# Three layers of attention on one core: self attentions in pairs between cross attentions, projections for two batches at once, tasks placed by a table

## The chip, the cores and the metric

The kernel runs on one core of a Trainium2 chip. The metric is the time of one execution in microseconds (us), on the device, as the median of several runs. A core has five engines that run side by side, each with its own instruction stream in order: TensorE (PE in the profile, with PEld for its weight loads), VectorE (DVE), ScalarE (ACT), GpSimd (POOL) and SyncE (SP), which here only starts DMAs. They meet at semaphores.

## The reference, cut to what matters

There are 8 batches of 112 tokens with 256 channels, and for each batch a context of 375 tokens. Everything is float32. One layer of cross attention is followed by a block with self attention, a second cross attention and an MLP.

```
# layer 0                                  16 heads of 16, softmax over 375 keys
xq, xkv = ada_ln(x, cond), ada_ln(ctx, cond)
x = x + mha(xq @ Wq + bq, k, v) @ Wp + bp          # k, v = xkv @ Wkv + bkv
# layer 1                                  self attention, 112 keys
h = ln(x) * (1 + scale_msa) + shift_msa            # shift, scale, gate = silu(cond) @ ada_w + ada_b
x = x + gate_msa * (mha(q, k, v) @ self_o_w + self_o_b)   # q, k, v = h @ qkv_w + qkv_b
# layer 2                                  cross attention, ctx is not normalised
x = x + mha((ln(x) * g2 + b2) @ q_w + q_b, k, v) @ cross_o_w + cross_o_b
# MLP, hidden 1024
x = x + gate_mlp * (gelu((ln(x) * (1 + scale_mlp) + shift_mlp) @ w1 + b1) @ w2 + b2)
```

Batches don't meet anywhere: batch b of layer 2 needs only batch b of layer 1, and so on.

## The kernel before, in words

**Attentions and steps.** There are 24 attentions: number i is layer i // 8, batch i % 8, and they run in that order, so the eight self attentions (8 to 15) stand in one block. `ORDER` (L58) is the list of steps that all five engine programs walk through: 3 x 12 steps ahead of attention 0 (FIRST = -3), then 12 steps for each cross attention and 4 for each self attention. In step u of attention i TensorE computes one unit of scores (`scores_t`, 4 matmuls, L477), ScalarE takes its exponential (`exponential`, L709, with the maximum already inside the product), and some steps later TensorE multiplies with the values (`values`, L522). Units share two PSUM banks, so unit n + 2 waits for the exponential of unit n.

**What an attention needs first.** The float32 product of queries and keys is made from bfloat16 parts: three parts each, six products stacked to a depth of 96, and three further rows that hold the negated maximum. So ahead of each attention comes a chain: the row maxima (`scores` L496 and L500 on TensorE, `maximum` L933 and L935 on VectorE: 16 for a cross attention, 4 for a self attention, two PSUM banks in turn), then `chain` (L943 to L949) that splits them, fill "N" (L603, L974) that transposes them, and a DMA by `load_maxima` (L1237) into the three rows of `q_stack`. The first unit of the attention waits for that DMA. For cross attentions `chain` is in step 8 and "N" in step 9 of the attention before; for self attentions in steps 0 and 1 of the attention before.

**Fills.** All other TensorE work between two attentions is cut into fills, each in one of two PSUM banks in turn (`fill`, `read`): "T" transposes half of a context, "K" projects half of its keys (L571, 375 columns), "V" its values (L577; two fills, of two and one blocks of 125 tokens), "X" transposes a normalised x, "Q" and "KS" project queries and self-attention keys of one batch (L594, 8 matmuls of 112 columns), "VS" self-attention values (L600), "A" and "B" prepare modulations and biases. The steps of the fills are written out by hand in tables (`NORM_AT`, `X_AT`, `Q_AT`, `T_AT`, `K_AT` and so on, L73 to L143).

**Jobs.** What "Q" and "KS" make is one job each, 32 in all: ScalarE writes it to `job_full` (L769), GpSimd splits it in four instructions (`split_job`, L1151 to L1157), and SyncE stacks it with six DMAs (`load_job`, L1232). Keys of a context go the same way (`split_keys` L1142 and L1144, `load_keys` L1222, 12 DMAs for an attention).

**Normalisation.** VectorE computes mean and variance (`norm` L924, L927; `context_stats` L911, L916), GpSimd the reciprocal root and the normalised rows (`norm` L1131 to L1137, `norm_context` L1118 to L1125).

**Start.** silu(cond) is computed on 8 partitions (`silu` L888 to L892), transposed by TensorE (L450) and used in L459; ScalarE starts all 17 small bias DMAs before its first activation. GpSimd waits for the bias rows (L1103) before it normalises anything.

**Other DMAs.** ScalarE's queue starts the contexts (`load_context`, L815, mostly in step 6 of an attention) and the weights; `wq`, `wkv` and `wo` are one buffer for layers 0 and 2.

**End.** After the last attention come the MLP's matmuls (`first_matmuls` L631, `second_matmuls` L641) for four pairs of batches.

Of the kernel before, what the change touches and what calls it, by code (L numbers as in the profile page):

```python
# [13 lines left out]
P = 128  # L14
# [19 lines left out]
QB = H * T + P - T  # L34
# [6 lines left out]
NA = 3 * B  # L41
FIRST = -3


def cross(i):
    return not B <= i < 2 * B


def steps(s):
    return 4 if B <= s < 2 * B else 12  # L50


def units(i):
    return 12 if cross(i) else 4


UNIT0 = [sum(units(j) for j in range(i)) for i in range(NA + 1)]
ORDER = [(s, u) for s in range(FIRST, NA) for u in range(steps(s))]  # L58

# [6 lines left out]
def cidx(i):  # L66
    return i if i < B else i - B


CROSS = [i for i in range(NA) if cross(i)]  # L70


NORM_AT, X_AT, Q_AT, KS_AT, VS_AT = {}, {}, {}, {}, {}  # L73
for p_, n_, x_, q_ in zip(range(B),
# [3 lines left out]
    NORM_AT[p_], X_AT[p_], Q_AT[p_] = n_, x_, q_  # L78
for b_ in range(B):
    p_ = B + b_  # L80
    if b_ < 6:
        NORM_AT[p_] = (b_ + 1, 10) if b_ else (2, 0)
        X_AT[p_], Q_AT[p_], KS_AT[p_], VS_AT[p_] = (b_ + 2, 3), (b_ + 2, 6), (b_ + 2, 8), (b_ + 2, 11)
    else:
        NORM_AT[p_] = (7, 10) if b_ == 6 else (9, 1)
        s_ = 8 if b_ == 6 else 10
        X_AT[p_], Q_AT[p_], KS_AT[p_], VS_AT[p_] = (s_, 0), (s_, 1), (s_, 2), (s_, 3)
    p_ = 2 * B + b_
    if b_ < 5:
# [12 lines left out]

T_AT, K_AT, V_AT = {}, {}, {}
for i_ in CROSS:
    T_AT[i_] = [(i_ - 3, 9), (i_ - 3, 10)]
    K_AT[i_] = [(i_ - 2, 0), (i_ - 2, 2)]
    V_AT[i_] = [(i_ - 1, 4), (i_ - 1, 5)]
T_AT[16], K_AT[16], V_AT[16] = [(9, 0), (9, 2)], [(11, 2), (11, 3)], [(12, 2), (12, 3)]
T_AT[17], K_AT[17] = [(13, 2), (13, 3)], [(14, 1), (14, 2)]
T_AT[18] = [(15, 1), (15, 2)]  # L110
STATS_AT = {i: [(i - 4, 8), (i - 4, 9), (i - 4, 10)] for i in range(B)}
STATS_AT[0] = [(-3, 1), (-3, 2), (-3, 3)]
XNC_AT = {i: (i - 3, 5) for i in range(B)}


MAX_AT, CHAIN_AT, N_AT = {}, {}, {}
for i_ in range(NA):
    if i_ == 2 * B:
        MAX_AT[i_] = [(14, k // 3) for k in range(12)] + [(15, 0)] * 4
        MAX_AT[i_] = [(13, 2), (13, 2), (13, 3), (13, 3)] + [(14, k // 3) for k in range(12)]  # L120
        CHAIN_AT[i_], N_AT[i_] = (15, 0), (15, 1)
    elif cross(i_):
        MAX_AT[i_] = [(i_ - 1, k // 2) for k in range(H)]
        CHAIN_AT[i_], N_AT[i_] = (i_ - 1, 8), (i_ - 1, 9)
    elif i_ == B:
        MAX_AT[i_], CHAIN_AT[i_], N_AT[i_] = [(7, k) for k in range(4)], (7, 4), (7, 5)
# [1205 lines left out]
```

## Time and profile before

| what | us |
|---|---|
| median of 3 runs (577.23 to 582.75) | 579.2 |
| the profiled execution, its own time | 582.22 |
| its span, first to last instruction | 580.4 |
| TensorE busy in the span | 467.1 |
| ahead of attention 0 | 80.87 |
| attentions 0 to 7 | 193.7 |
| self attentions 8 to 15 | 94.75 |

The profile is of one execution. Its own time is 1.8 us above its span and 3.0 us above the median of the runs. The attention stretches are read from the first L477 of each attention in the timeline: 80.87, 274.57 and 369.32 us.

### The profile page before, as it was taken

To read this page: it belongs to the slowest core of one execution; us is meant where nothing else is said; L and a number is where in the kernel's file an instruction comes from. 1 tells how busy PE (TensorE), PEld (TensorE's weight loads), DVE (VectorE), ACT (ScalarE), POOL (GpSimd) and SP (SyncE) were. 2 spreads that over 40 slices of the span, in tenths; PEclk is the share of its full clock that TensorE was granted. 3 is DMA by queue.
4 is the path that set the end of the run, shared out by engine and by line. 5 is a ranking of instruction groups with operands and counts; after the bars stand their busy time and mean duration, and the time that the engine had idled before them with its cause. 6 is when DMAs were issued, how large, how long until landed. Compare 5 with 4: busy or idle time off the path is not lost.

```text
span 580.4 us, 11962 instructions
## 1 busy us (share of the span) xinstructions
PE 467.1 (80%) x4446; PEld 342.5 (59%) x4446; DVE 255.4 (44%) x682; ACT 244.6 (42%) x537; POOL 262.1 (45%) x406
## 2 busy tenths in 40 slices
PE   0554769696989999968787866999699998989996
PEld 0432547464656676657665654666466655659885
DVE  0521713445455555535354475546266556622112
ACT  0121132343555655545453343555355555466220
POOL 5444642887585573443446535644223423143000
PEclk9995857888799999998797899899899999799999
DMA  8723421323243434342522422424613231100001
GB/s 207 179 61 95 130 77 29 100 70 81 75 130 96 123 93 110 88 126 81 137 75 58 107 53 64 131 52 124 176 43 96 52 82 46 38 2 1 17 16 33
DMA packets 74786, 48.70 MB, mean 84 GB/s; under 512 B 38968, under 2 KB 71696, under 8 KB 74728
## 3 DMA queue, kind: packets, MB, share of 16 engines
q1 hardware_dynamic: 65804, 38.08, 25.4%
q10 hardware_dynamic: 8924, 9.85, 5.8%
q8 instruction: 36, 0.59, 0.4%
q14 instruction: 22, 0.18, 0.1%
HBM read 17.27 MB, written 0.93 MB: 31 GB/s over the span
## 4 chain that ended last, share of the span: by engine, by line
PE 60%; DVE 11%; DMA 9%; POOL 8%; issue 5%; SPq 4%; ACT 2%; ACTq 0%; POOLq 0%; DVEq 0%
PE bank L571 9%; DMA q_stack<-nm_t 8%; DVE nmax L933 7%; PE bank L522 7%; PE bank L577 7%; PE bank L477 6%; PE bank L496 6%; PE bank L594 6%; PE bank L641 5%; PE bank L631 4%; PE bank L543 3%; POOL ctx_norm L1125 3%; PE bank L531 2%; POOL x_norm L1137 1%; SPq L873 1%
## 5 line engine op out<-in xcount | busy, mean ns | idle before, releaser
L933 DVE TENSOR_REDUCE nmax<-bank 112x1 f32<-112x375 f32 x256 | 127.9, 543 | 157.4 <-PE bank L496 157.2
L709 ACT ACTIVATE prob<-bank 125x448 f32<-125x448 f32 (+1 forms) x224 | 120.1, 544 | 136.4 <-PE bank L477 119.9
L477 PE MATMUL bank<-q_stack,k_stack 99*128 99x112 bf16 x768 | 73.0, 222 | 24.3 <-DMA q_stack<-nm_t 16.2
L496 PE MATMUL bank<-k_stack,q_stack 96*128 96x375 bf16 x256 | 75.2, 346 | 17.5 <-DVE nmax L933 8.1
L477 PEld LDWEIGHTS bank<-q_stack,k_stack 99*128 99x128 bf16 x768 | 52.0, 103 | 48.4 <-DMA q_stack<-nm_t 19.5
L571 PE MATMUL bank<-ctx_t,wkv 128*128 128x375 f32 x128 | 59.7, 599 | 2.8 <-ACT ctx_t L730 1.8
L496 PEld LDWEIGHTS bank<-k_stack,q_stack 96*128 96x128 bf16 x256 | 25.6, 102 | 54.9 <-DVE nmax L933 34.2
L1131 POOL TENSOR_SCALAR x_veps<-x_mv 112x1 f32<-112x1 f32 x32 | 7.4, 233 | 105.7 <-DVE x_mv L927 105.2
L522 PE MATMUL bank<-prob,v_tokens 125*17 125x112 f32 x1536 | 52.2, 271 | 0.1
L1142 POOL CAST k_parts<-k_rest 128x375 bf16<-128x375 f32 x32 | 16.0, 499 | 79.3 <-DVE k_rest L983 79.3
L577 PE MATMUL bank<-wkv,ctx_t 128*125 128x256 f32 x192 | 49.9, 397 | 0.0
L522 PEld LDWEIGHTS bank<-prob,v_tokens 125*17 125x17 f32 x1536 | 34.7, 100 | 15.9 <-issue 12.9
L1137 POOL TENSOR_SCALAR x_norm<-x_tokens,x_mv,x_rstd 112x256 f32<-112x256 f32 x32 | 39.6, 1237 | 3.3
L935 DVE TENSOR_REDUCE nmax<-bank 112x4 f32<-112x448 f32 x32 | 19.8, 624 | 41.4 <-PE bank L500 41.2
L577 PEld LDWEIGHTS bank<-wkv,ctx_t 128*125 128x125 f32 x192 | 34.9, 195 | 4.2
L571 PEld LDWEIGHTS bank<-ctx_t,wkv 128*128 128x128 f32 x128 | 26.7, 231 | 15.9 <-issue 6.0
L1151 POOL CAST job_part<-job_full 128x224 bf16<-128x224 f32 x32 | 12.1, 378 | 52.8 <-ACT job_full L769 52.7
L739 ACT ACTIVATE k_parts<-bank,bias_heads 128x375 bf16<-128x375 f32 x32 | 18.4, 575 | 36.5 <-PE bank L571 36.5
L1125 POOL TENSOR_SCALAR ctx_norm<-ctx_tokens,ctx_mv,ctx_rstd 125x256 f32<-125x256 f32 x24 | 29.6, 1242 | 0.8
L1144 POOL TENSOR_TENSOR k_parts<-k_rest,k_parts 128x375 bf16<-128x375 f32 x32 | 27.3, 852 | 2.6
L641 PE MATMUL bank<-late_space,k_self_stack 128*112 128x256 f32 x128 | 28.1, 379 | 0.0
L769 ACT ACTIVATE job_full<-bank,bias_heads 128x112 f32<-128x112 f32 x64 | 19.2, 352 | 19.3 <-PE bank L594 19.2
(114 smaller groups left out, 753.4 us busy)
## 6 DMA issues: line engine op xcount, KB each, us to landing
k_stack<-k_parts SPq DMA_DIRECT2D x192, 93.8 KB, 2.2
q_stack<-job_part SPq DMA_DIRECT2D x144, 56.0 KB, 2.0
ctx_tokens<-in_ctx_dram ACTq DMA_DIRECT2D x14, 375.0 KB
k_self_stack<-job_part SPq DMA_DIRECT2D x48, 56.0 KB, 2.0
late_space<-in_L_xcond_mlp_w_dram ACTq DMA_DIRECT2D x2, 1024.0 KB, 5.3
late_space<-in_L_xcond_ada_w_dram SPq DMA_DIRECT2D x1, 1536.0 KB, 6.2
gate_self<-gate_rows SPq DMA_DIRECT2D x8, 112.0 KB, 3.7
k_self_stack<-gate_rows SPq DMA_DIRECT2D x1, 896.0 KB, 7.0
```

The source lines that it names most:

```text
L477: last = pe.matmul(sh.score_t[n % 2][:, j * T:(j + 1) * T], keys, sh.q_all[:, b, o:o + T], start=True, stop=True)
L496: last = pe.matmul(bank[:, 0:L], sh.q_all[0:DEEP, b, place(k) * T:place(k) * T + P], sh.k_st[i % 2][0:DEEP, k, 0:L], start=True, stop=True)
L522: last = pe.matmul(sh.pv[32 * j:32 * j + D + 1, g * T:(g + 1) * T], v, sh.prob[n % NPROB][0:rows, j * T:(j + 1) * T], start=t == 0, stop=t ...
L571: last = pe.matmul(cx[:, 0:L], w[:, c, n * P:(n + 1) * P], sh.ct[i % 2][:, c, :], start=c == 0, stop=c == CH - 1)
L577: last = pe.matmul(cx[0:KT, (t % 2) * C:(t % 2 + 1) * C], sh.ct[i % 2][:, c, t * KT:(t + 1) * KT], sh.wkv[i // B][:, c, C:2 * C], start=c ...
L594: last = pe.matmul(cx[:, m * T:(m + 1) * T], sh.wq[i // B][:, c, at + m * P:at + (m + 1) * P], sh.xt[i % 2][:, c, :], start=c == 0, stop=c ...
L641: last = pe.matmul((sh.pv, sh.tb)[j][0:T, 0:C], sh.hid[p % 2][:, m, j * T:(j + 1) * T], sh.w2[:, m, :], start=m == 0, stop=m == NH - 1)
L709: act.activation(sh.prob[n % NPROB][0:rows, :], sh.score_t[n % 2][0:rows, 0:GH * T], ACT.Exp, scale=SCALE).then_inc(sg.exp_done, 1)
L933: dve.tensor_reduce(sh.nmax[i % 2][:, place(k):place(k) + 1], sh.score[n % 2][0:T, 0:L], AX_X, ALU.max, negate=True).then_inc(sg.max_done, 1)
L1125: pool.tensor_scalar(sh.xnc[:, t, :], sh.ctx[r][:, t, :], sh.ctx_mv[:, j, t, 0:1], sh.ctx_rstd[:, j, t:t + 1], ALU.subtract, ALU.mult).the ...
L1137: pool.tensor_scalar(sh.xn[j][:, :], sh.x[:, b, :], sh.mv[:, j, 0:1], sh.rstd[:, j:j + 1], ALU.subtract, ALU.mult).then_inc(sg.xn_done, 1)
L1144: pool.tensor_tensor(sh.kp[par][:, 2, m, :], sh.kr[:, m, :], sh.kp[par][:, 1, m, :], ALU.subtract).then_inc(sg.split[m], 1)
```

## The change

The order of the attentions becomes a list, `SEQ`. Steps are numbered by one integer g: 17 ahead of the first attention (`PRE`) instead of 36, then 12 or 4 for each as before. The hand-written tables give way to functions: `put` fixes a task in a step, `lightest` picks in a given range of steps the one with the least TensorE time by a table of costs (`LOAD`), and `spread_sp` deals the DMAs of a job or of keys out two to a step. "Q" and "KS" take two batches at once: 16 jobs in place of 32, each twice as wide (224 columns), the two batches side by side in `q_stack`. "V" is three fills of one block. The normalised x (all of it) and the first two contexts move from GpSimd to VectorE. Contexts are loaded 2 or 3 steps after the buffer is free; silu is computed transposed from a transposed load of cond; of the small bias DMAs all but four start after the exponential of silu; the first job is stacked from ScalarE's queue. Layers 0 and 2 get their own weight buffers. The MLP's matmuls are as before.

```diff
-QB = H * T + P - T
+QP = H * 2 * T + P - T
...
+SEQ = ([(0, b) for b in range(5)] + [(1, 0), (1, 1), (0, 5), (0, 6), (1, 2), (1, 3), (0, 7)]
+       + [(2, 0), (1, 4), (1, 5), (2, 1), (2, 2), (1, 6), (1, 7)] + [(2, b) for b in range(3, 8)])
...
+PRE = 17
+START = [PRE + n for n in UNIT0]
...
+def lightest(lo, hi, cost, *task):
+
+    g = min(range(lo, hi + 1), key=lambda g: (LOAD[g] + 0.02 * (g - lo), g))
+    return put(g, *task, cost=cost)
...
+    TAIL_AT[i] = [end + 3, end + 5, end + (8 if nxt == 12 else 6)]
...
+    CHAIN_AT[i], N_AT[i] = (12, 13) if i == 0 else (START[i] - 4, START[i] - 3)
...
+for ci in range(2, NC):
+    g = cross_start(ci - 2)
+    k0 = lightest(g + 1, g + 2, 1.27, "K", ci, 0)
+    K_AT[ci] = [k0, lightest(k0 + 2, g + 5, 1.27, "K", ci, 1)]
...
+for lay in (1, 2, 3):
+    for b in sorted(range(B), key=lambda b: POS[lay - 1, b]):
+        i = POS[lay - 1, b]
+        g = NORM_AT[lay, b] = TAIL_AT[i][2] + 1
...
+        X_AT[lay, b] = lightest(g + 3, g + 4, 0.22, "X", (lay, b), 0)
+        if lay < 3 and b % 2:
+            x = max(X_AT[lay, b], X_AT[lay, b - 1])
+            q = Q_AT[lay, b - 1] = lightest(x + 2, x + 3, 1.5, "Q", (lay, b - 1), 0)
+            if lay == 1:
+                ks = KS_AT[lay, b - 1] = lightest(q + 2, q + 4, 1.5, "KS", (lay, b - 1), 0)
...
+def spread_sp(g, *what):
+    for part in range(3):
+        while g >= PRE and SP_LOAD[g] >= 2:
+            g += 1
+        put_sp(g, *what, part)
+    ISSUED[what] = g
...
             for m in range(CH):
                 for c in range(CH):
-                    last = pe.matmul(cx[:, m * T:(m + 1) * T], sh.wq[i // B][:, c, at + m * P:at + (m + 1) * P], sh.xt[i % 2][:, c, :],
-                                     start=c == 0, stop=c == CH - 1)
+                    last = pe.matmul(cx[:, m * 2 * T:(m + 1) * 2 * T], sh.wq[lay][:, c, at + m * P:at + (m + 1) * P],
+                                     sh.xt[PAIR_NO[i] % 2][:, c, :], start=c == 0, stop=c == CH - 1)
...
+        if g == 4:
+            act.wait_ge(sg.job_step, 4)
+            for part in range(3):
+                stack_job(act, sh, sg, JOBS[0], part)
...
+    weights_at = {5: (0, "wo"), 9: (2, "stage"), 12: (3, "stage"), START[0] + 3: (1, "wv"), START[0] + 9: (1, "wo"),
+                  START[2] + 5: (4, "stage"), START[2] + 10: (5, "stage"), START[3] + 3: (2, "wv"), START[3] + 8: (2, "wo"),
+                  START[6] + 1: (0, "mlp"), START[7] + 4: (1, "mlp")}
+    for ci in range(2, NC):
+        context_at[T_AT[ci - 2][1] + (3 if ci >= B + 2 or ci < 4 else 2)] = ci
...
+    act.wait_ge(sg.cond_in, 32)
+    act.activation(sh.exp_t[:, :, :], sh.cond_t[:, :, :], ACT.Exp, scale=-1.0).then_inc(sg.exp0, 1)
     small_loads(act, sh, sg, ins)
...
     def norm(p):
+        lay, b = p
+        n = NORM_NO[p]
+        dve.wait_ge(sg.xn_rstd, n + 1)
+        if n >= 3:
+            wait_filled(dve, sg, ("X", NORM_ORDER[n - 3], 0))
+        dve.tensor_scalar(sh.xn[n % 3][:, :], sh.x[:, b, :], sh.mv[:, n % 2, 0:1], sh.rstd[:, n % 2:n % 2 + 1],
+                          ALU.subtract, ALU.mult).then_inc(sg.xn_done, 1)
...
+        for p in NORMS.get(g, []):
+            if NORM_NO[p] >= 2:
+                norm_stats(p)
+        for p in NORMS.get(g - 2, []):
+            if NORM_NO[p] >= 2:
+                norm(p)
...
+        if g == START[NA - 5] + 4:
+            sp.wait_ge(sg.st_psum, max(UNIT0[POS[1, b] + 1] for b in range(4, B)))
             sp.dma_start(sh.gate_m, gate_rows[:, 1, :].partition_broadcast(T)).then_inc(sg.gate_m_in, 16)
```

GpSimd keeps the variance's reciprocal root (`rstd`, in its loop one step after VectorE's statistics), the splitting of keys and jobs, the other six contexts' normalisation, and the bias additions.

## Rows read from the trace of the kernel before

**Rows 1.** The page: busy time of three engines, and the granted clock in 40 slices

```profile
PE 467.1 (80%) x4446; PEld 342.5 (59%) x4446; DVE 255.4 (44%) x682; ACT 244.6 (42%) x537; POOL 262.1 (45%) x406
PEclk9995857888799999998797899899899999799999
```

**Rows 2.** Windows: from:to length, busy (count) of PE, PEld, DVE, ACT, POOL; clock; DMA

```profile
0.00:80.87 80.87, 36.67 (x131) 25.69 (x132) 23.46 (x73) 13.93 (x28) 40.11 (x63) 0.83 0.51 131
80.87:148.25 67.38, 54.67 (x447) 38.64 (x448) 27.37 (x82) 24.93 (x54) 42.90 (x59) 0.78 0.26 69
195.88:217.32 21.44, 20.09 (x219) 14.40 (x220) 11.28 (x28) 12.03 (x27) 13.60 (x21) 1.00 0.40 106
274.57:369.32 94.75, 72.15 (x732) 54.83 (x731) 46.47 (x123) 40.69 (x95) 50.73 (x85) 0.89 0.33 87
454.12:473.46 19.34, 17.78 (x199) 11.86 (x200) 11.16 (x28) 10.54 (x23) 6.83 (x11) 1.00 0.25 63
511.50:522.38 10.88, 9.45 (x183) 6.89 (x184) 1.72 (x5) 7.51 (x17) 5.64 (x9) 1.00 0.01 2
522.38:580.40 58.02, 53.56 (x268) 47.95 (x267) 9.91 (x25) 15.99 (x35) 5.54 (x8) 0.98 0.06 17
```

**Rows 3.** Chain that ended last, its start: from us, for us, what

```profile
17.02 5.68 DMA bias_rows<-in_L_xcond_mlp_b_dram
...
44.77 3.64 POOL ctx_norm L1125 x3
...
51.17 0.60 SPq L1232
...
74.44 6.38 DMA q_stack<-nm_t
```

**Rows 4.** The same chain later: pieces at the full clock, and DMA waits

```profile
190.88 0.94 PE bank L594 x8
...
408.17 5.89 DMA q_stack<-nm_t
...
439.06 1.32 PE bank L571 x4
...
442.62 1.79 PE bank L577 x8
...
450.08 0.70 PE bank L522 x24
451.89 2.19 DMA q_stack<-nm_t
...
529.20 6.81 PE bank L631 x36
```

**Rows 5.** Groups by shape: count, busy us, mean ns, idle before

```profile
L496 PE MATMUL bank<-k_stack,q_stack 96*128 96x375 bf16 x256 | 75.2, 346 | 17.5 <-DVE nmax L933 8.1 <-DMA q_stack<-job_part 2.2 <-DVE nmax L935 1.1
L1137 POOL TENSOR_SCALAR x_norm<-x_tokens,x_mv,x_rstd 112x256 f32<-112x256 f32 x32 | 39.6, 1237 | 3.3
L1144 POOL TENSOR_TENSOR k_parts<-k_rest,k_parts 128x375 bf16<-128x375 f32 x32 | 27.3, 852 | 2.6
L1153 POOL TENSOR_TENSOR job_rest<-job_full,job_part 128x224 f32<-128x224 f32 x32 | 19.6, 612 | 2.6
L1013 DVE TENSOR_SCALAR late_space<-bank,mod 128x112 f32<-128x112 f32 x4 | 1.4, 389 | 9.2 <-PE bank L582 9.2
L888 DVE TENSOR_SCALAR late_space<-late_space 8x256 f32<-8x256 f32 x1 | 0.3, 280 | 14.4 <-ACT late_space L824 14.4
```

**Rows 6.** What TensorE waited for: us in total, times, longest

```profile
PE bank L450 <- DVE late_space L892: 18.4, 1, 18.4
PE bank L477 <- DMA q_stack<-nm_t: 17.4, 13, 4.2
```

**Rows 7.** Timeline, two engines side by side at 26 us

```profile
26.64 4.04 POOL L1125 TENSOR_SCALAR ctx_norm<-ctx_tokens,ctx_mv,ctx_rstd 125x256 f32<-125x256 f32 x3
26.67 0.65 DVE L1039 COPY wkv<-k_self_stack 128x256 f32<-128x256 f32 x2
```

More of the change, by code:

```diff
@@ new lines, with cross_start, put @@
+SELF_NO = {i: n for n, i in enumerate(j for j in range(NA) if not cross(j))}
+PRE = 17
+START = [PRE + n for n in UNIT0]
+END = START[NA]
+STEP_OF = {START[i] + u: (i, u) for i in range(NA) for u in range(steps(i))}
+def cross_start(ci):
+    return START[CROSS[ci]] if ci >= 0 else {-1: 4, -2: 1, -3: 0}[ci]
+LOAD = [0.0] * (END + 40)
+TASKS = {}
+def put(g, *task, cost=0.0):
+    TASKS.setdefault(g, []).append(task)
+    LOAD[g] += cost
+    return g
+def lightest(lo, hi, cost, *task):
+    g = min(range(lo, hi + 1), key=lambda g: (LOAD[g] + 0.02 * (g - lo), g))
+    return put(g, *task, cost=cost)
@@ new lines @@
+for i in range(NA):
+    for u in range(steps(i)):
+        LOAD[START[i] + u] += 0.2
+MAX_AT, CHAIN_AT, N_AT, VALUES_AT, TAIL_AT, K_LAND = {}, {}, {}, {}, {}, {}
+for i in range(NA):
+    end = START[i + 1]
+    if cross(i):
+        VALUES_AT[i] = [[START[i] + 4, START[i] + 7, START[i] + 10, end + 1][u // 3] for u in range(12)]
+    else:
+        VALUES_AT[i] = [[START[i] + 3, end + 1][u // 2] for u in range(4)]
+    for g in sorted(set(VALUES_AT[i])):
+        LOAD[g] += 0.9 if cross(i) else 0.6
+    nxt = steps(i + 1) if i + 1 < NA else 12
+    TAIL_AT[i] = [end + 3, end + 5, end + (8 if nxt == 12 else 6)]
+    for g, cost in zip(TAIL_AT[i], (0.44, 0.2, 0.86)):
+        LOAD[g] += cost
@@ new lines @@
+for i in range(NA):
+    CHAIN_AT[i], N_AT[i] = (12, 13) if i == 0 else (START[i] - 4, START[i] - 3)
+for i in range(NA):
+    for g in range(CHAIN_AT[i] - 8, CHAIN_AT[i]):
+        LOAD[g] += 0.32 if cross(i) else 0.11
+    put(N_AT[i], "N", i, 0, cost=0.1)
+T_AT, K_AT, V_AT, STATS_AT, XNC_AT = {}, {}, {}, {}, {}
+T_AT[0], K_AT[0], V_AT[0] = [0, 0], [1, 2], [9, 10, 11]
+T_AT[1], K_AT[1] = [3, 3], [4, 5]
+for kind, at in (("T", T_AT), ("K", K_AT), ("V", V_AT)):
+    for ci, where in list(at.items()):
+        for n, g in enumerate(where):
+            put(g, kind, ci, n, cost={"T": 0.33, "K": 1.27, "V": 0.86}[kind])
@@ new lines, with invert @@
+B_AT = [7, START[1] + 3, START[4] + 8]
+for n, g in enumerate(B_AT):
+    put(g, "B", n, 0, cost=0.43)
+A_AT = [START[0] + 2, START[0] + 6]
+for n, g in enumerate(A_AT):
+    put(g, "A", n, 0, cost=2.0)
+FILL_RANK = {k: n for n, k in enumerate(("N", "K", "X", "Q", "KS", "VS", "V", "T", "B", "A"))}
+FILLS = {g: sorted(t, key=lambda f: FILL_RANK[f[0]]) for g, t in TASKS.items()}
+FILL_NO = {}
+for g in sorted(FILLS):
+    for f in FILLS[g]:
+        FILL_NO[f] = len(FILL_NO)
+def invert(table, many=False):
+    found = {}
+    for key, where in sorted(table.items(), key=lambda kw: kw[1] if not many else kw[1][0]):
+        for n, g in enumerate(where if many else [where]):
+            found.setdefault(g, []).append((key, n) if many else key)
+    return found
@@ new lines @@
+for g in SP_AT:
+    SP_AT[g].sort(key=lambda w: w[0] != "N")
+for i in range(NA):
+    last = CHAIN_AT[i] - 1
+    if i == 0:
+        MAX_AT[i] = [5 + k // 2 for k in range(H)]
+        continue
+    lay, b = SEQ[i]
+    ready = ISSUED.get(("J", ("Q", (lay, b - b % 2), 0)), 4) + 3
+    if cross(i):
+        ci = CIDX[i]
+        first = max(ISSUED.get(("K", (ci, 0)), 9) + 3, ready)
+        second = max(ISSUED.get(("K", (ci, 1)), 11) + 3, first + 2)
+        MAX_AT[i] = [first + (second - first) * k // HC for k in range(HC)] + \
+            [last - (last - second + 1) * (HC - 1 - k) // HC for k in range(HC)]
+    else:
+        MAX_AT[i] = [last - 3 + k for k in range(4)]
@@ L229 @@
+MAXES, MAX_NO = invert(MAX_AT, True), {}
+for g in sorted(MAXES):
+    for m in MAXES[g]:
+        MAX_NO[m] = len(MAX_NO)
+N_MAX = len(MAX_NO)
 MODS = [1.0, 0.0, 1.0, 0.0, 0.0, 1.0, 0.0, 1.0]
@@ L1147, in split_job @@
         j = JOB_NO[f]
-        full, part = sh.full[j % 2], sh.part[j % 2]
+        full, part = sh.full, sh.part[j % 2]
         wait_read(pool, sg, f)
```

797 lines of the change are left out of this document (377 added, 420 removed), and 3 rows, old and new, of the table CROSS.

## The prediction
> **What bounds the kernel now.** I read four views in this order: the page, the windows by stretch, the chain that ended last, and the groups by shape. The page shows TensorE busy 467.1 of 580.4 us and no other engine above 262 [rows 1]; the slices of granted clock fall below full speed at the start and around the self attentions. The windows say where TensorE isn't well used [rows 2]. A cross attention of layer 2 takes 19.34 us, 17.78 of them busy at the full clock: that stretch is bound by TensorE. But 80.87 us pass before attention 0, with 36.67 busy; attentions 0 and 1 take 67.4 us at a mean clock of 0.78; the eight self attentions and the fills between them take 94.75 us with 22.6 idle and a clock of 0.89. The MLP, 58.0 us, is full. So there is a stretch that can only shrink by less work (TensorE's own), and three that lose time to latency. The chain names what is late at the start: a bias row for GpSimd until 22.70 (17.02 + 5.68), two context normalisations of about 4 us on GpSimd, six stacking DMAs at 0.6 us each, and 6.38 us from the issue of the maxima's DMA to its landing, where the same DMA takes 2.19 later [rows 3, 4].
>
> **Part 1: the start.** Before, TensorE waits 18.4 us for silu [rows 6], because 17 DMA issues stand ahead of ScalarE's exponential. After, four do. The modulations still wait for all small loads, which now are issued later; they landed about 21 us before and I take 24. That holds VectorE's queue (x norm, weight order, second statistics stand behind), so the first context is on TensorE at 25 to 27 us and not at 30.7 (the end of GpSimd's normalisation, 26.64 + 4.04) [rows 7]. Two key halves and the paired query projection at the low clock end near 37.5. The normalisation moved to VectorE is bounded by 0.28 and 0.63 us: L888 reads 280 ns, and L1013 389 ns for 112 columns, up to 0.63 if the whole difference from a tiny instruction (some 0.2) grows with width [rows 5]; I take 0.35. What matters more is that GpSimd splits the first job at once instead of after the second context's 3.64 us, which ended at 48.41, with stacking at 50.6 and landing at 55.7 [rows 3]. A job twice as wide costs GpSimd more: from 224 to 375 columns an instruction grows from 612 to 852 ns [rows 5], 1.6 ns a column, so 970 ns at 448, a factor of 1.58 on 2.2 us: 3.4 us. 37.5 + 0.8 (ScalarE's read) + 3.4 + six issues of 0.6 + 2 landing = 47.5, 8 us earlier. From there 16 maxima at 0.55 us of VectorE (8.8), interleaved with two X, a Q of two batches, V and B, take about 16 us, four maxima of attention 1 stand ahead of the split of attention 0's maxima (+2), and the DMA takes 2.2 instead of 6.4 since no context or weight is loaded beside it. First unit at about 68: 13 us gained. Bounds 62 (modulations ready at once, clock high) and 76 (small loads land at 30).
>
> **Part 2: work on TensorE.** A projection of one batch is 0.94 us; eight matmuls of 224 columns are, by 36 of them in 6.81 us, 1.51 [rows 4]. Two batches cost 1.51 instead of 1.88: 0.37 x 16 = 5.9 us saved; one pair lies in the start, where it only shortens the latency. The three V fills do the same matmuls as two did. Weight buffers of their own remove waits that were not late.
>
> **Part 3: the body, by prices.** I price all that stands between the first unit and the MLP, at the full clock. A cross attention's own units: values 4 x 0.70 [rows 4], scores 12 x 0.25 (eight matmuls in 0.50), tail 1.5, so 7.3; 16 maxima 16 x 0.346 [rows 5] = 5.5; keys 2 x 1.32; values projection 1.79 + 0.92 [rows 4]; T 0.65, X 0.35, N 0.2. With K, V, T, X, N and maxima that is 19.3 for the full stretch, which lasted 19.34 [rows 2]; with the Q, KS and VS of layer 1 it is 22.1, where 21.44 was measured: the prices hold to 3%. After: 16 x 7.3 = 116.8; 15 sets of maxima less ten done in the start, 79; 14 K 37.0; 15 V 40.5; 13 T, 26 X, 23 N 22; 14 paired projections 21.1; 8 VS 7.2; 8 self attentions at 4.6 (values 1.0, scores 1.0, tail 1.5, four maxima 1.1) 36.8; A and B 8.2; 2.9 because the last attention has no fills beside it (10.88 for 7.3, less what overlaps) [rows 2]. Sum 371.5. The same list before is 381, and the stretch from 80.87 to 522.38 took 441.5: 60 us lie in waits and in the low clock.
>
> **Part 4: how much of the 60 goes.** By place: attentions 0 and 1 hold 17 (67.4 against 50 by price), the self stretch 27 (94.75 against 67.8), the rest 16, among them two waits of 5.9 for the maxima's DMA where 2.2 is normal [rows 4]. Why the self stretch is late: maxima, split, transpose, DMA and first unit follow one another within four short steps, and there is too little other work. After, self attentions come in twos with the keys, values and projections of cross attentions around them, the maxima of the second one are made during the cross attention before, and I take 2 us left for each pair, 8 in all. Attentions 0 and 1 keep 6: GpSimd is no longer ahead of every X, but A still needs 6.4 us of TensorE in attention 0. Of the rest 6 stay. SyncE loses 96 of 192 job issues, at 0.64 us with the gap about 61 us of its queue, and the maxima's DMA stands first in its step with at most two issues ahead. Contexts are loaded near step 1 and not 6, away from the maxima's DMA in step 9; `gate_m` goes five steps ahead of it. One collision stays, `w1` (1 MB) in the same step as attention 7's maxima: 3.7 us by the difference of 5.89 and 2.19. Sum 20 left. What is late next is TensorE itself, 17.8 of 19.3 us busy.
>
> **Added waits.** VectorE now waits for GpSimd's root (`rstd`) two steps after its statistics; behind that wait stand the maxima, and TensorE's score banks wait for them. GpSimd needs 0.8 us for the root, but a job (3.4) or a context (3.64 plus its root) can stand ahead. Two steps are about 3.2 us, so I count this as hidden, and its failure is a rival. GpSimd itself is relieved: 39.6 us for x, a quarter of the context rows, and 19 us of the jobs go.
>
> There is a row for interference: GpSimd's three normalisations took 4.04 us beside VectorE's 0.65 us of copies, and 3.64 without [rows 3, 7]. The Trainium skill, "SBUF — State Buffer", section "Who interferes with whom", says that VectorE and GpSimd share a pair of ports, and that a tensor_scalar between SBUF buffers can take it whole while GpSimd stands still, or the other way round. The trace agrees by 0.4 us. By that rule each of the 32 moved norms could cost VectorE up to one GpSimd instruction, which makes the rival with the late VectorE likelier.
>
> **Sum.** 68 + 371.5 + 20 + 58 = 517.5 us of span, 519.3 as the profiled execution (1.8 outside the span), and 3.0 less on the scale of the median: forecast **517**, against 579.2.
>
> **Rivals.**
> - All latency is hidden: 62 + 371.5 + 5 + 58 = 496.5, 496 on the median's scale. For it speaks that every fill finds a step with little load; against it that even the fullest stretch idles 1.6 of 19.3 us. Chance 0.15.
> - The self attentions keep their latency: the four dependent links are the same per attention, and in twos the second has only four steps. If 20 of the 27 us stay in place of 8, and half of the start's gain fails, 517 + 12 + 7 = 536. For it speaks that nothing in the chain of links gets shorter. Chance 0.2.
> - The new order only moves the waits, and the change brings its start and its fewer projections alone: 579.2 - 13 - 6 = 560. For it speaks that maxima and fills still alternate in two banks each. Chance 0.08.
> - Slower: VectorE waits for GpSimd's root at every norm. The price is one GpSimd job ahead, 3.4 us, and the ports; TensorE has two score banks and loses it all. With 28 norms after the start a mean wait of 2.2 us eats the whole gain of 62 us; with 3.4 it is 95, so 612. Against it: only 14 jobs and 6 contexts lie in the body, so few norms can meet one. Chance 0.04.
> - The table doesn't do what it says: key DMAs and jobs, two issues a step, miss the step from which the maxima are placed, and TensorE stands at each. At 3 us for each of 20 attentions the gain is gone: 577. Chance 0.03.
>
> The forecast, within 500 to 530, has 0.5. Its range by itself is 500 to 530; the range for 8 in 10 is **498 to 548**. A measurement of this kernel can tell about 1% from no change: faster by over 1% 0.93, within 1% 0.03, slower 0.04.
>
> **What would show it.** Right: first L477 at 62 to 76 us; projections of 224 columns near 0.19 us each, 128 records less; stretches of a full cross attention near 20 us, a pair of self attentions with the fills near 16; `q_stack<-nm_t` waits of TensorE well below 17.4 us; mean clock above 0.916; TensorE busy about 440 us. Wrong: waits of VectorE for GpSimd's `x_rstd` of more than 20 us in total, a start above 76 us because the small loads land late, or idle of TensorE in the self pairs above 5 us each. If TensorE's busy time doesn't fall although its clock rises, the prices of part 3 were not what it pays.

## Result: slower, and the profile after

The kernel after takes 595.8 us (median of 4 runs, 595.3 to 602.2) against 578.2 for the kernel before beside it on the same chip: ratio 1.033, 95% interval 1.022 to 1.043. The forecast was 517, in a range of 498 to 548. The prediction was wrong, in its sign too. In all times and ratios here and below, executions over 1.5% above the fastest one of the same kernel are left out as slow.

The page of after, with busy time and granted clock, to be held against [rows 1]:

```profile
span 592.6 us, 11515 instructions
...
PE 459.1 (77%) x4316; PEld 333.4 (56%) x4316; DVE 273.9 (46%) x719; ACT 241.2 (41%) x521; POOL 201.8 (34%) x304
...
PEclk9998776979999797999869998898869999899999
```

TensorE lost 8 us of work and GpSimd 60, as the change meant, and the span of the profiled executions grew by 12 (by the medians it is 17.5; before's profiled execution was 4 us above its median). So time went into idle of TensorE. The windows of after (columns as in [rows 2]) say where: ahead of attention 0, attentions 0 and 1, a cross attention of layer 2, all attentions together, the MLP.

```profile
0.00:82.27 82.27, 35.60 (x134) 23.78 (x134) 29.19 (x85) 13.85 (x29) 29.49 (x51) 0.89 0.55 132
82.27:141.66 59.39, 47.81 (x421) 33.03 (x420) 25.79 (x79) 24.02 (x52) 29.37 (x41) 0.84 0.24 66
461.44:482.68 21.24, 18.27 (x208) 13.31 (x206) 12.09 (x30) 11.11 (x26) 8.72 (x13) 1.00 0.24 60
82.27:532.60 450.33, 368.62 (x3894) 260.87 (x3896) 233.54 (x607) 210.37 (x457) 165.16 (x242) 0.91 0.31 82
532.60:592.60 60.00, 54.91 (x294) 48.79 (x294) 11.12 (x27) 16.93 (x36) 7.20 (x12) 1.00 0.05 16
```

The same stretch of all attentions in the kernel before:

```profile
80.87:522.38 441.51, 376.86 (x4048) 268.91 (x4049) 222.02 (x584) 214.70 (x475) 216.43 (x337) 0.92 0.32 84
```

TensorE is busy for 368.62 us between the first unit and the MLP. But it stands still for 81.7 us there (450.33 - 368.62), before 64.7 (441.51 - 376.86). The start didn't get shorter: 82.27 for 80.87. The stretch of layer 2 does the same tasks as the one of before in [rows 2] and one paired query projection more. It takes 21.24 us for 19.34, with 2.97 idle and not 1.56, all at the full clock.

What TensorE waited for, in after (us in total, times, longest):

```profile
PE bank L631 <- DVE x_norm L995: 39.8, 23, 8.2
PE bank L655 <- DVE nparts L1018: 32.5, 22, 2.4
PE bank L508 <- DVE silu_t L947: 17.5, 1, 17.5
PE bank L546 <- DVE nmax L1002: 11.5, 35, 0.6
PE bank L546 <- DMA q_stack<-job_part: 10.9, 2, 10.2
PE bank L550 <- DMA k_self_stack<-job_part: 4.8, 1, 4.8
```

and in before:

```profile
PE bank L603 <- DVE nparts L949: 14.8, 10, 2.6
PE bank L560 <- POOL ctx_norm L1125: 12.2, 2, 7.5
...
PE bank L582 <- POOL x_norm L1137: 6.2, 4, 2.6
```

The wait for the maxima's DMA, 17.4 us in [rows 6], is gone (0.3 in after). Two waits for VectorE took its place: for the normalised x (L631, before L582) 39.8 us for 6.2, and for the split maxima (L655, before L603) 32.5 for 14.8. VectorE itself isn't full, 46%. The timeline of after inside another cross attention of layer 2 shows both. First the norm:

```profile
450.27 0.55 DVE L1002 TENSOR_REDUCE nmax<-bank 112x1 f32<-112x375 f32 x1 [1.42 <-PE bank L546]
...
450.73 0.60 DVE L1051 SCALAR_TENSOR_TENSOR k_rest<-bank,bias_heads,k_parts 128x375 f32<-128x375 f32 x1
...
451.25 0.40 DVE L995 TENSOR_SCALAR x_norm<-x_tokens,x_mv,x_rstd 112x256 f32<-112x256 f32 x1
...
451.80 0.38 PE L631 MATMUL bank<-ident,x_norm 112*128 112x112 f32 x2 [1.18 <-DVE x_norm L995]
```

The root was ready at 449.81 (`x_rstd`, 449.24 + 0.57), and VectorE stood idle for 1.42 us. But its program puts the norm at the end of the step, behind a maximum and the reading of keys that TensorE makes in that same step. When it is done, TensorE has already come to the transpose that needs it, and has lost 1.18 us. Then the chain:

```profile
455.34 1.03 PE L593 MATMUL bank<-wo,ot 128*112 128x256 f32 x4
...
456.41 0.42 DVE L1035 TENSOR_TENSOR gated<-bank,gate_self 112x256 f32<-112x256 f32 x1 [2.15 <-PE bank L593]
...
456.87 0.42 DVE L1037 TENSOR_TENSOR x_tokens<-gated,x_tokens 112x256 f32<-112x256 f32 x1
457.21 0.17 DVE L1012 CAST nparts<-nmax 112x16 bf16<-112x16 f32 x1
...
457.83 0.17 DVE L1018 TENSOR_TENSOR nparts<-nrest,nparts 112x16 bf16<-112x16 f32 x1
458.12 0.10 PEld L655 LDWEIGHTS bank<-ident_bf,nparts 112*48 112x48 bf16 x1 [1.71 <-issue]
458.15 0.21 PE L655 MATMUL bank<-ident_bf,nparts 112*48 112x112 bf16 x1 [1.58 <-DVE nparts L1018]
```

All 16 maxima come from earlier steps; the chain needs nothing from this step. But the table puts the third tail step (`end + 8`) in the step that is also the chain's (`START[i] - 4` is step 8 of 12), and VectorE's loop does the tail before the chain. So the chain waits 2.15 us for an output projection with which it has nothing to do, and TensorE loses 1.58. In the kernel before the tail stood one step ahead, in step 7. The Trainium skill, "Perfetto Trace Analysis", section "Tensor Engine Instruction (MATMUL, LD_WEIGHTS)", says that the queues of VectorE, ScalarE and GpSimd are strict: an instruction doesn't overtake one that waits. The trace agrees: VectorE is idle for 2.15 us, with the chain, whose inputs were there, behind the tail.

The start's chain of after, cut to what matters here (columns as in [rows 3]; of the issues of the small loads two are shown):

```profile
1.20 15.25 DMA cond_t<-in_cond_dram
17.19 0.61 ACTq L920
...
26.21 0.62 ACTq L921
26.87 4.70 DMA norm_b<-in_L_xcond_norm_b_dram
...
52.31 6.59 DMA q_stack<-job_part
```

The condition is now loaded transposed, elements of 4 bytes one by one, and lands at 16.45; before, silu came at 18.97. So silu is only 1.5 us earlier (17.4). But 14 small loads are now issued behind the exponential and the last lands at 31.6, where before they were all there at 21.3. The modulations wait for them.

### The profile page after: what moved, and what is told of

The parts are those of the page before. It is cut to its first block, busy times and chain, and to the rows that moved or that the text cites. A ratio compares the mean times of both kernels' runs of the same rounds, so it can differ in the third digit from the quotient of the medians.

```text
span 592.6 us, 11515 instructions
## 1 busy us (share of the span) xinstructions
PE 459.1 (77%) x4316; PEld 333.4 (56%) x4316; DVE 273.9 (46%) x719; ACT 241.2 (41%) x521; POOL 201.8 (34%) x304
## 2 busy tenths in 40 slices
DMA packets 63022, 48.65 MB, mean 82 GB/s; under 512 B 14928, under 2 KB 59936, under 8 KB 62968
## 3 DMA queue, kind: packets, MB, share of 16 engines
q1 hardware_dynamic: 51116, 37.38, 24.5%
## 4 chain that ended last, share of the span: by engine, by line
PE 64%; DVE 17%; DMA 6%; issue 5%; POOL 3%; ACTq 2%; SPq 2%; ACT 1%; DVEq 0%; POOLq 0%
PE bank L572 8%; PE bank L626 7%; DVE nmax L1002 7%; PE bank L621 7%; PE bank L526 6%; PE bank L546 6%; PE bank L645 5%; PE bank L693 5%; PE bank L683 4%; PE bank L593 3%; DMA cond_t<-in_cond_dram 3%; PE bank L581 2%; DVE x_norm L995 2%; PE bank L652 2%; SPq L1317 2%
## 5 line engine op out<-in xcount | busy, mean ns | idle before, releaser
L1002 DVE TENSOR_REDUCE nmax<-bank 112x1 f32<-112x375 f32 x256 | 131.0, 543 | 170.4 <-PE bank L546 169.0
L546 PE MATMUL bank<-k_stack,q_stack 96*128 96x375 bf16 x256 | 80.7, 353 | 24.4 <-DVE nmax L1002 11.5
L621 PE MATMUL bank<-ctx_t,wkv 128*128 128x375 f32 x128 | 53.9, 549 | 2.7 <-ACT ctx_t L778 1.8
L626 PE MATMUL bank<-wkv,ctx_t 128*125 128x256 f32 x192 | 53.3, 400 | 0.1
L631 PE MATMUL bank<-ident,x_norm 112*128 112x112 f32 x64 | 13.5, 296 | 39.8 <-DVE x_norm L995 39.8
L792 ACT ACTIVATE v_tokens<-bank 125x256 f32<-125x256 f32 x48 | 18.5, 385 | 41.7 <-PE bank L626 41.1
L631 PEld LDWEIGHTS bank<-ident,x_norm 112*128 112x128 f32 x64 | 7.2, 153 | 44.7 <-issue 36.4
L621 PEld LDWEIGHTS bank<-ctx_t,wkv 128*128 128x128 f32 x128 | 24.5, 213 | 13.5 <-issue 4.2
L655 PE MATMUL bank<-ident_bf,nparts 112*48 112x112 bf16 x24 | 5.3, 219 | 32.5 <-DVE nparts L1018 32.5
L693 PE MATMUL bank<-late_space,q_stack 128*112 128x256 f32 x128 | 28.1, 379 | 0.0
L683 PE MATMUL bank<-late_space 128*128 128x224 f32 x128 | 25.3, 353 | 0.0
```

What stands on the lines that cost most here:

```text
L546: last = pe.matmul(bank[:, 0:L], sh.q_all[0:DEEP, b // 2, o:o + P], sh.k_st[CIDX[i] % 2][0:DEEP, k, 0:L], start=True, stop=True)
L621: last = pe.matmul(cx[:, 0:L], w[:, c, n * P:(n + 1) * P], sh.ct[i % 2][:, c, :], start=c == 0, stop=c == CH - 1)
L626: last = pe.matmul(cx[0:KT, 0:C], sh.ct[i % 2][:, c, n * KT:(n + 1) * KT], sh.wkv[0 if i < B else 2][:, c, C:2 * C], start=c == 0, stop=c ...
L631: last = pe.transpose(cx[:, c * T:(c + 1) * T], sh.xn[NORM_NO[i] % 3][:, c * P:(c + 1) * P], sh.ident[0:T, 0:T])
L683: last = pe.matmul((sh.score + sh.score_t)[n % 4][:, 0:2 * T], sh.w1[:, c, m * P:(m + 1) * P], sh.xtm[:, c, 2 * p * T:2 * (p + 1) * T], st ...
L693: last = pe.matmul((sh.pv, sh.tb)[j][0:T, 0:C], sh.hid[p % 2][:, m, j * T:(j + 1) * T], sh.w2[:, m, :], start=m == 0, stop=m == NH - 1)
```

## Experiments

Edits are against the kernel after, if not said otherwise. Times are medians, the interval (95%) is that of the ratio to the kernel before beside it, whose median was 576.3 to 578.3 in the groups of runs.

**One part each: chain, norm, both, small loads.** First VectorE's chain ahead of its tail:

```
-        for i, k in TAILS.get(g, []):
-            tail(i, k)
         for i in CHAINS.get(g, []):
             chain(i)
+        for i, k in TAILS.get(g, []):
+            tail(i, k)
```

> The changed kernel with one edit: in VectorE's step the split of the maxima stands before the attention's tail and not behind it. Theory W (the loss is waits that come from a task's place in an in-order stream; the new table puts the third tail step into the step of the split, so fill N waits for the out-projection): TensorE's wait for nparts at fill N falls from 32.5 us to under 8, no wait takes its place, and the time falls by 15 to 25 us, to about 576. Rival M (the waits only move: some other dependency holds the same step): the wait at N falls, others rise by as much, and the time stays within 5 us of 596. Rival S (all of the loss is the start and the slow small loads): no change.

Measured 569.4 us, ratio 0.987 (0.981 to 0.993): 26.4 us less than after, from the order of two calls. TensorE's wait for `nparts` fell by half, to 16.6 us (12 times), and not under 8 as expected; the wait for `x_norm` grew by 3.7 us, to 43.5. Then VectorE's norm at the head of its step:

```
     for g in range(END):
+        for p in NORMS.get(g - 2, []):
+            if NORM_NO[p] >= 2:
+                norm(p)
         for f in FILLS.get(g, []):
...
-        for p in NORMS.get(g - 2, []):
-            if NORM_NO[p] >= 2:
-                norm(p)
```

> The changed kernel with one edit: VectorE's normalisation of x stands at the head of its step, before that step's maxima, and not at its end, where it waits for TensorE's scores and key fills of the same step. Theory W: TensorE's wait for x_norm at fill X falls from 39.8 us to about 12 (8.2 of it are in the start), the time falls by 15 to 25 us, to about 576; VectorE waits for GpSimd's x_rstd a little more than the 8.9 us of now, under 15. Rival M: the wait turns into one of VectorE for x_rstd (over 25 us) and the time stays within 5 us of 596. Rival S: no change.

Measured 579.3, ratio 1.005 (1.001 to 1.009), 16.5 us less than after. TensorE's wait for `x_norm` fell to 21.1 and not to 12. VectorE's for the root rose to 32.2, which was the sign of rival M (over 25); but the time that M gave, within 5 us of 596, didn't come. With both edits:

> Both edits at once. Theory W: they are separate waits, so the gains add, 35 to 45 us, to about 555, below the kernel before. Rival M: less than 10 us in all. Halfway, if the same slack serves both: about 570.

Measured 561.6, ratio 0.975 (0.968 to 0.983). Together they gain 34 us, a little under the 35 to 45 expected, where the two alone gave 43 (26.4 + 16.5). What the two changed in TensorE's waits, by kernel (e2_norm_head, then e12_both, which differ by the chain), and last VectorE's own wait for the root in e12_both, which was 8.9 us in after:

```profile
PE bank L655 <- DVE nparts L1018: 32.2, 23, 2.4
PE bank L631 <- DVE x_norm L995: 21.1, 9, 8.1
```

```profile
PE bank L631 <- DVE x_norm L995: 23.8, 10, 7.8
...
PE bank L655 <- DVE nparts L1018: 16.9, 13, 2.4
...
DVE x_norm L995 <- POOL x_rstd L1216: 34.3, 26, 5.1
```

VectorE stands four times as long for GpSimd's root, and the kernel is 34 us faster: here the place of an instruction in VectorE's queue costs time, and VectorE's own idle time much less.

All small loads ahead of the exponential:

```
+    small_loads(act, sh, sg, ins)
     act.wait_ge(sg.cond_in, 32)
     act.activation(sh.exp_t[:, :, :], sh.cond_t[:, :, :], ACT.Exp, scale=-1.0).then_inc(sg.exp0, 1)
-    small_loads(act, sh, sg, ins)
```

> The changed kernel with one edit: the 14 small bias loads are issued before ScalarE waits for cond, not after the exponential. Theory S for the start: the first modulation waits for the last small load, which lands at 31.6 us; issued early it lands at about 23, the exponential is about 2 us later, and the first unit of attention 0 comes at 75 instead of 82.3: the time falls by 6 to 8 us. Rival: the start is then held by something else (the landing of the first job at 58.9 beside key DMAs and a context, or the key fills), and the time falls by under 2 us.

Measured 590.2, ratio 1.024 (1.016 to 1.032). The small loads landed at 25.2, but ScalarE was held by its issues until 22.2, silu came at 24.5 and the first unit at 81.2, not at 75. One wait took the other's place. The time is 5.6 us less than after's all the same, which looks like the 6 to 8 expected but isn't that: only 1.1 us lie in the start. The granted clock was 0.928 to 0.933 in these runs and 0.909 to 0.922 in after's; whether the edit has to do with that isn't shown.

**The mirror, on the kernel before.** If tail and chain in one step cost the kernel after about 26 us, putting them in one step must cost before a similar time.

```
-        TAIL_AT[i_] = [(nxt, 3), (nxt, 5), (nxt, 7)]
+        TAIL_AT[i_] = [(nxt, 3), (nxt, 5), (nxt, 8)]
```

> The kernel before with one number changed: the output projection of the attention that ended (third tail step) in step 8 of a cross attention and not in step 7, so that it stands in the same step as the chain that splits the next attention's maxima, as the table of the kernel after has it. Theory (VectorE does the tail first in a step, so the chain waits for the output projection, and the transpose that TensorE does at the head of the next step waits for the chain): TensorE's wait for nparts rises from 14.8 us (10) to 30 to 36 us (24 to 26), each new one about 1.2 us; median 588 to 596, ratio 1.02 to 1.03. Rival (the wait of after comes from the shorter attentions and the fuller steps, not from the two standing in one step): nparts waits stay below 20 us, ratio within 1% of 1.

Measured 596.8, ratio 1.031 (1.025 to 1.036): one number in the table of before costs 18.5 us, as much as the whole loss of after. The wait went from 14.8 us (10 times), by 16.6, to

```profile
PE bank L603 <- DVE nparts L949: 31.4, 23, 2.2
```

Then the edit of e1_chain_first in the kernel before:

```
-        for i, k in TAILS.get((s, u), []):
-            tail(i, k)
         for i in CHAINS.get((s, u), []):
             chain(i)
+        for i, k in TAILS.get((s, u), []):
+            tail(i, k)
```

> The kernel before with VectorE's chain ahead of its tail in each step, as in e1_chain_first. There the two stand in one step only around the self attentions (10 waits for nparts, 14.8 us). Theory: these waits shrink to 5 or less, and the time falls by 6 to 10 us, ratio 0.983 to 0.99, all of it between attentions 7 and 16. Rival (in short steps the chain is late because its last maximum is late): the wait stays above 11 us and the ratio within 0.5% of 1.

Measured 574.3, ratio 0.991 (0.987 to 0.996): 4 us less, not 6 to 10. The wait fell to 6.2 (8), but the wait for the maxima's DMA rose, from 17.4 to 26.5. To see whether more of it can be had in before, the chain at the head of its step there:

```
     for s, u in ORDER:
+        for i in CHAINS.get((s, u), []):
+            chain(i)
...
-        for i in CHAINS.get((s, u), []):
-            chain(i)
```

> The kernel before with VectorE's chain at the head of its step, as e15_chain_at_head has it, and nothing else. It says what order, pairs and table are worth when both kernels have this repair. Theory (the new order shortens the chain of dependent links of the self attentions and the pairs save projections, as the forecast had it): before gains little from the repair, 4 to 9 us as e10_before_chain_first did, because its tail stands one step ahead of the chain in the long steps and its transfers of the maxima are late; 568 to 574, so that 30 us or more lie between it and e15_chain_at_head. Rival (the gain of e15_chain_at_head is the repair alone and the new order brings nothing): 545 to 560, nparts below 4 us and waits for nm_t not above 18.

Measured 576.6, ratio 0.999 (0.994 to 1.003). Nothing is left of the repair:

```profile
PE bank L477 <- DMA q_stack<-nm_t: 28.7, 16, 6.1
...
PE bank L603 <- DVE nparts L949: 2.2, 2, 1.8
```

In before the DMA of the maxima is the next thing late: its wait grew by 11.3 us where the one for `nparts` fell by 12.6. So the theory's number didn't hold (it isn't 568 to 574), but the rival that the repair alone makes the gain (545 to 560) is out.

**The start.** On top of e12_both, the start of before: condition as eight rows of 1 KB, silu on eight partitions, two transposes and a copy, all small loads first.

```
-        for k in range(CH):
-            act.dma_start(sh.cond_t[:, k, :], ins["cond_1024"][:, k * P:(k + 1) * P].rearrange("b p -> p b"))...
+    act.dma_start(sh.cond[0][:, :], ins["cond_1024"]).then_inc(sg.cond_in, 16)
...
+            last = pe.transpose(sh.tb[:, k * B:(k + 1) * B], sh.cond[1][:, k * P:(k + 1) * P], sh.ident[0:B, 0:B])
```

> Both moves of e12_both kept (chain ahead of the tail, VectorE's norm at the head of its step), and the start of the kernel before put back: the condition loaded as eight rows of 1 KB, exponential and silu on eight partitions, two transposes on TensorE and a copy; all 16 small loads issued ahead of the exponential. Theory (the 4-byte transposed load of the condition lands at 16.5 us and what is issued behind it on the same queue is held back, so the small loads land at 31.6 and not at 21): small loads back near 21 to 22, modulations near 23 to 25 although silu comes at 19 and not at 17.4, first unit of attention 0 at 73 to 76 where e12_both had 80.3; median 554 to 557 against 561.6. Rival (the first unit hangs on the first job's DMAs, which land late because twelve key DMAs, a context and a weight are moved beside them): modulations early, but the job still lands at 57 or later and the first unit at 79 to 81; median 560 to 562.

Measured 553.1, ratio 0.958 (0.952 to 0.964). The small loads were there at 21.3, the first unit came at 73.51 and not at 80.3. Load, silu and the place of the small loads were changed at once, so this run doesn't tell them apart; e3_small_first says that the place of the small loads alone doesn't bring it. ScalarE's queue at the start, first in after, then here (start, length):

```profile
0.72 1.08 ACTq L904 DMA_DIRECT2D cond_t<-in_cond_dram  x2
1.83 5.18 ACTq L905 DMA_DIRECT2D bmod<-in_L_xcond_bss_kv_dram  x1
```

```profile
0.72 0.59 ACTq L906 DMA_DIRECT2D late_space<-in_cond_dram  x1
1.34 0.41 ACTq L908 DMA_DIRECT2D bmod<-in_L_xcond_bss_kv_dram  x1
```

The same load of 2 KB takes 5.18 us to issue behind the transposed loads and 0.41 behind the plain one.

**GpSimd or VectorE.** e1_chain_first with the norm back on GpSimd, right behind its root.

```
         for p in NORMS.get(g - 1, []):
             if NORM_NO[p] >= 2:
                 rstd(p)
+                norm(p)
```

> The chain ahead of the tail as in e1_chain_first, and the x norm back on GpSimd right behind its root, in the step after the statistics (the statistics stay on VectorE). Theory A (what costs is that VectorE and GpSimd hand the norm back and forth, each through its own queue): VectorE's waits for x_rstd vanish (10.8 in e1_chain_first, 34.3 in e12_both), TensorE's wait for x_norm falls from 43.5 us to below 24, and the median is at or below 561.6 of e12_both. Theory B (GpSimd is the slower and fuller engine, and 28 norms of about 0.9 us come on it and stand ahead of its key splits and jobs): wait for x_norm above 24 us or waits for q_stack and k_stack DMAs that grow by 5 us or more, median 563 to 572.

Measured 559.6, ratio 0.969 (0.963 to 0.975); e12_both had 561.6, ratio 0.975 (0.968 to 0.983), so the two can't be told apart. By its waits this is between the two theories: 25.5 us for GpSimd's `x_norm` and 7.9 for the one in the start. So moving the norms to VectorE wasn't what brought the gain. On GpSimd they also stand a step earlier; the engine alone, at the same step, wasn't tried.

**What is left in VectorE's order.** On top of e5_start_as_before, the chain at the head of its step (attention 0 excepted, whose maxima share its step); the norm three steps behind its statistics, with the transposes one step later; and both. The first three lines are e15_chain_at_head, the others e57_norm_a_step_later.

```
+        for i in CHAINS.get(g, []):
+            if i > 0:
+                chain(i)
...
-        for p in NORMS.get(g - 2, []):
+        for p in NORMS.get(g - 3, []):
-        X_AT[lay, b] = lightest(g + 3, g + 4, 0.22, "X", (lay, b), 0)
+        X_AT[lay, b] = lightest(g + 4, g + 5, 0.22, "X", (lay, b), 0)
```

> e5_start_as_before, with VectorE's chain of splits at the head of its step (before the maxima and the readings of that step) and not behind them; all its maxima lie in earlier steps. Theory (the 16.6 us, 13 times, for nparts that are left come from the chain standing behind a maximum and the reading of a fill that TensorE makes in the same step): this wait falls below 5 us and the time by 8 to 12 us, to 541 to 545. Rival (VectorE is then late with the maximum behind the chain, 0.8 us later, and TensorE waits for its score banks instead: nmax, 10.3 us, grows by as much): nparts below 5, nmax above 18, time 550 to 553.

Measured 537.5, ratio 0.932 (0.924 to 0.940): 15.6 us less, more than the 8 to 12 expected. The wait fell by 10.8 us (16.6 to 5.8), and the rest goes with the clock. Three of the four runs had 0.940 to 0.949, against 0.919 to 0.929 in e5_start_as_before. The fourth, at 0.927, took 542.1 us, and the run of e5_start_as_before at 0.929 took 552.3: 10.2 us at the same clock, about the wait that is gone. Attention 0 in e5_start_as_before and in e15_chain_at_head, with the same work and nearly the same idle time (4.6 and 5.1 us), at a granted clock of 0.73 and 0.88:

```profile
73.51:105.63 32.12, 27.50 (x209) 18.79 (x208) 10.90 (x38) 11.43 (x25) 12.01 (x18) 0.73 0.19 51
```

```profile
73.61:102.21 28.60, 23.51 (x208) 16.41 (x207) 10.80 (x38) 11.28 (x25) 12.07 (x18) 0.88 0.21 57
```

These 3.5 us are no wait of anything, and the edit leaves attention 0 out. That it caused them, or the higher clock, isn't shown.

> e5_start_as_before, with VectorE's norm three steps after the statistics and not two, and the transposes of x at the fourth or fifth step and not the third or fourth. Theory (VectorE stands 34 us, 26 times, at the head of its step for a root that GpSimd computes only after its own work of the steps before, and TensorE loses 15.3 us for x_norm and part of the 10.3 for nmax to that): VectorE's wait falls below 12 us, TensorE's for x_norm below 11 (8 of it in the start), time 546 to 549. Rival (the loop from a tail over norm, projection and stacking to the scores of the next layer is as short as the table allows; one step more makes the jobs late): waits of TensorE for q_stack or k_self_stack grow by over 3 us in the body, time 553 to 560.

Measured 544.9, ratio 0.948 (0.941 to 0.955); VectorE's wait for the root fell to 10.6, TensorE's for `x_norm` to 10.6, of which 7.4 lie ahead of 127 us. No wait of the jobs grew by over 1 us; the start grew by 1.9 (first unit at 75.45).

> The edits of e15_chain_at_head and e57_norm_a_step_later together. If both causes are as stated and lie at different places, the gains add: 16.6 + 7 less what the clock or the banks take back, 534 to 541 us. If they are the same slack of VectorE seen twice, the pair is no better than the better one of the two alone by over 2 us.

Measured 530.8, ratio 0.921 (0.916 to 0.926): 6.8 us under the better of the two, and below the 534 to 541 expected. This version beats both kernels, before by 47 us and after by 65.

The path from after to it, by medians: chain ahead of the tail 26.4, norm at the head of its step 7.7 (16.5 if it comes first), the old start 8.5, chain at the head 15.6, norm a step later 6.8; 65.0 in all. The runs of one kernel lie up to 8 us apart, so the single shares are good to a few us. No edit changes what is computed or the order of the attentions.

## Why the prediction was wrong

The span of each part as forecast, as measured in after, and in e15_chain_at_head (e15). The windows of e15, the second one over the same tasks as after's stretch of layer 2 above, are

```profile
0.00:73.61 73.61, 36.76 (x135) 24.90 (x136) 31.43 (x86) 13.96 (x29) 30.05 (x51) 0.88 0.59 148
...
413.82:432.80 18.98, 18.37 (x207) 13.23 (x206) 12.25 (x29) 11.10 (x26) 8.71 (x13) 1.00 0.26 68
73.61:477.55 403.94, 358.14 (x3894) 253.31 (x3896) 232.19 (x607) 208.88 (x457) 164.00 (x242) 0.94 0.34 91
477.55:537.60 60.05, 54.92 (x295) 48.79 (x294) 11.12 (x27) 16.94 (x36) 7.19 (x12) 1.00 0.06 16
```

| part | forecast | after | e15 |
|---|---|---|---|
| ahead of attention 0 | 68 | 82.3 | 73.6 |
| attentions | 391.5 | 450.3 | 403.9 |
| MLP | 58 | 60.0 | 60.1 |
| span | 517.5 | 592.6 | 537.6 |

- **Part 4 failed: "Sum 20 left" of latency in the attentions.** It was 78.8 (450.3 - 371.5), with TensorE idle for 81.7 us. I argued about links, engines and queues and counted a task as hidden if its step had room. I didn't place the tasks in VectorE's queue, where tail, chain and norm stand in an order written in the loop. That `end + 8` and `START[i] - 4` are the same step, and that the tail comes first, can be read from the diff. The three edits of VectorE's order alone took back 26.4 + 7.7 + 15.6 us.
- **"Added waits" was right in its number and wrong in what follows.** VectorE waits 8.9 us for GpSimd's root, as few as I thought (the bound was 20). I took that for the norm being hidden. But the norm's cost was on the other side, at whoever waits for it: TensorE, 39.8 us. I priced what is queued behind the new wait, and not what the new instruction is queued behind. The rival with the root (612) had the sign right and the mechanism wrong: with 34.3 us of that wait e12_both is 34 us faster than after. The ports were of little weight as well: the 32 norms took 15.3 us together, the median one 0.405 and the longest 1.27, so by estimate 2.3 us in all were lost beside other work (15.3 - 32 x 0.405).
- **Part 1 failed: the start at 68.** It had two terms off. The small loads land at 31.6 and not at 24, because 14 of them wait for the exponential, and that for the condition, which lands at 16.5. The sum has no term for the condition's load and goes by the issues ahead of the exponential; four do remain, but they end only at 8.8. And the first job's DMAs take 6.59 us from the last issue to landing, not 2; with the old start (e5_start_as_before) they still take 6.64. They now go beside twelve key DMAs and a context, but that this is the reason wasn't tried. With the old start the first unit came at 73.5, inside the bounds of 62 to 76. That is not the gain as forecast: silu and small loads are there as in before, so the earlier exponential has no part in it. Splitting the paired job took GpSimd from 45.18 to 48.54, 3.36 us, as priced (3.4).
- **Part 2 was a little too large.** In the chain of after, the view from which I had the 0.94 us of a single projection, eight matmuls of 224 columns take 1.57 or 1.58 us at the full clock, not 1.51 as I had from 36 others. The pair saves 0.30 us and not 0.37, so 4.8 us and not 5.9 over 16:

```profile
171.23 1.57 PE bank L645 x8
```

- **Part 3 came close in part by luck.** 371.5 us were priced and 368.6 were busy, but these are not the same thing: the prices are of the full clock and hold the small gaps of a full stretch, and the busy time is at a granted clock of 0.91, without gaps. At 0.94, in e15, the same matmuls were busy for 358.1. The full stretch of layer 2 with a paired projection took 18.98 us in e15, where the prices give 20.8 (19.3 + 1.5). So they were somewhat high, and the low clock filled the difference.
- **The relief of SyncE held:** TensorE's waits for the maxima's DMA went from 17.4 us to 0.3, and the collision with `w1` did not show.
- **The change does bring time once its queue is in order, if less than forecast.** With its chain at the head of the step the kernel before stays at 576.6 (e16_before_chain_at_head), and e15 has 537.5. These 39 us are what the rest of the change is worth together: the order, the pairs, the table, the start as far as e15 has it, the norms and their place. No run parts them. Self attentions in pairs are not as cheap as I had them: 2 us left for each, and near 16 us with their fills. In after the four pairs take 20 to 28 us with 4 to 6 us idle, at a granted clock of 0.66 to 0.86 where I priced the full one. The sign that I named (over 5) came in two of them:

```profile
284.60:312.34 27.74, 22.19 (x170) 15.43 (x167) 11.76 (x31) 9.49 (x22) 9.52 (x13) 0.75 0.31 82
353.64:378.55 24.91, 19.16 (x170) 13.54 (x167) 11.67 (x31) 9.36 (x22) 9.52 (x13) 0.86 0.31 81
```

The sum gives 516.3 on the scale of the median (519.3 - 3.0) and was written down as 517; that changes nothing. The 4% for slower was far too little. Of the signs that the prediction listed, "a start above 76 us because the small loads land late" came true in after; but e3_small_first, where they land early, has its first unit at 81.2 too. TensorE's busy time, 459.1 us, stayed above the 440 that was named as a sign of being right. What stays open: the last 14 us between e157_both_later and the forecast (in e15, which is 20 above: 5.6 in the start, 12.4 in the attentions, 2 in the MLP), what moves the granted clock from run to run, and the order of the attentions by itself, which wasn't tried.

## What to carry to other kernels

When a table or a planner moves tasks between steps, write down for one step the real queue of every engine, in program order, and ask of each instruction which foreign result stands ahead of it; "there is room in the step" doesn't answer that. On an engine that works in order, what only needs old results belongs at the head of the step, what needs this step's results at its end. A small wait of the engine you moved work to doesn't clear the move: look for who waits for it.

## What the runs showed of the hardware

- Two loads of 4 KB each, gathered in elements of 4 bytes, landed 6.9 and 15.3 us after their issue and held the queue behind them: the next issue took 5.18 us where it takes 0.41 behind a plain load of 8 KB. The Trainium skill, "DMA: Bandwidth & Descriptors", section "Why small descriptors are slow (HBM only)", counts an overhead per packet and per descriptor; the direction agrees. The two loads are 2048 elements, and e5_start_as_before, which differs from e12_both in the start alone, has 12856 packets under 512 bytes and not 14928: 2072 fewer.
- The granted clock differs between runs of one kernel, and the time with it: e15_chain_at_head took 535.5 us at 0.949 and 542.1 at 0.927. Between it and e5_start_as_before, 10.8 us of a wait were removed and the median fell by 15.6; at like clocks (0.927 and 0.929) it fell by 10.2. In attention 0 the same work with as much idle took 28.60 us at 0.88 and 32.12 at 0.73.
- With the norms on VectorE (0.40 us each) or on GpSimd (1.24 [rows 5]) and a step earlier, the time was the same within the intervals (561.6 and 559.6).
